# Spline-compressed FFN behind cross attention, one core: gate and up weights as one stationary matrix per tile, down cells in four classes, half of the rounding on ScalarE

## The chip, the core and the metric

The kernel runs on one core of one Trainium2 chip. The metric is the time of one execution on the device in microseconds (us). The kernel before takes 267.11 us, the median of three runs (267.0 to 267.25).

## What is computed

Four batches of 512 tokens with 512 columns. Each batch goes through an attention whose weights come from a context, and then through a feed-forward network whose three weight matrices are not stored: they are cubic (Catmull-Rom) interpolations of some 8000 control points each. Cut to what matters:

```python
x = x + xattn(layernorm(x), ctx, Wq, bq, Wk, bk)
#   query, key = ctx @ Wq.T + bq, ctx @ Wk.T + bk;  attention = softmax(query @ key.T)
#   xattn = layernorm(x) mixed by attention
gate_w = spline_reconstruct(gate_cp, 2048, 512)   # one control interval spans about 129 weights
up_w   = spline_reconstruct(up_cp, 2048, 512)
down_w = spline_reconstruct(down_cp, 512, 2048)
h = layernorm(x)
x = x + (silu(h @ gate_w.T) * (h @ up_w.T)) @ down_w.T
```

## The kernel before

All tensors are 128 partitions wide; a "tile" below is 128 of the 2048 inner rows (16 tiles, m = 0 to 15) by 512 tokens. The order of the work is written out by hand. One list of stages, `attention_only` and then `ffn(st, b, a)`, is run through once for each engine, and an engine issues its own part of each stage in that order. `ffn(b, a)` does the feed-forward network of batch b and, in between, the attention of batch a = b + 1. Between engines there are only semaphores; on one engine everything is first in, first out.

**Prologue.** `attention_only` makes the weights and does the attention of batch 0. An interpolated weight matrix is split into a smooth part of low rank ("nodes") and a residual that is not zero only near the breaks of the spline. The residual is a product of a small matmul (`spread`, L1209 to L1227) with precomputed tables: `residual` on VectorE multiplies two banks with two tables (L876), on GpSimd adds the two products (L1049). This gives gu_r for gate and up (8 steps, 512 wide) and d_r for down (8 steps of two tiles, 2 x 192 wide). `node_weights` (L1257, L717, L896) gives the node part gu_v. The table of down is loaded only when the gate and up residuals are done (L615).

**Gate and up, `gate_up(b, m)`.** Each of the two sums of a tile takes two matmuls: the residual weights against 128 columns of h (L1327) and 102 rows of node weights against zg, the projection of h on the node functions (L1330). ScalarE applies Silu out of the PSUM bank (`activate`, L776), VectorE multiplies with the up bank (L964), GpSimd rounds the product to fp32r for the down matmuls (`round_inter`, L1124). Gate and up have two banks each: gate(m) waits for the Silu of m - 2, up(m) for the product of m - 2.

**The projection.** `project` (L1306, L762, L952) makes zp from h; `replicate` (L1313, L769, L956) spreads it once to zg.

**Down.** `down_basis` (L1344) and `gather_halves` (L1356) take the node part, `down` (L1372) the residual part: per tile and token quarter one matmul of 128 rows against 192 columns. `down_tail` (L1379) adds the node part, and VectorE adds the result to x (L991).

**Attention inside `ffn`.** `energy` (L1192), `softmax` (maxima on VectorE L853, Exp on ScalarE L683), `scale` (L860), `prob_t` (transposes, L1236), `split_prob` (L703, L883). `split_x` splits the transposed input into xh (ScalarE, L709) and xl (VectorE, L887); `xm` (48 matmuls, L1279 to L1281) waits for it. Then `add_xm`, `norm_t` (transposes, L1294), and `cast_t`: ScalarE copies a bank to SBUF (L752), VectorE makes a rounded copy of that (L945). `project` of the next batch waits for all four ScalarE copies (L1301).

The stretch of `ffn` from the last tiles on, in the order in which all engines take it:

```python
st.activate(b, 15); st.round_inter(b, 15)
st.split_prob(a, 3); st.split_x(a)
st.down(b, 0, range(0, 12)); st.down_basis(b, 1); st.down(b, 0, range(12, 13))
st.down_basis(b, 2); st.half_split(b)
st.down(b, 0, range(13, 16)); st.down(b, 1, range(0, 16))
st.stats(a); st.xm(a, 0)
```

## Time and profile before

| | |
|---|---|
| median of three runs | 267.11 us |
| span of the profiled execution, first to last instruction | 265.8 us |
| TensorE matmuls busy | 247.6 us, 93% |
| VectorE | 188.2 us, 71% |
| GpSimd | 132.2 us, 50% |
| ScalarE | 123.6 us, 46% |
| start of `project`, batches 0 to 3 | 65.47, 119.68, 172.80, 225.92 us |

The profiled execution has no time of its own beside its span; the median of the runs is 1.3 us longer than the span, for what lies before the first and behind the last instruction. PE is TensorE, DVE is VectorE, ACT is ScalarE, POOL is GpSimd. A row of a timeline has the start, the duration, the engine, the line and the operation; "x2" is two instructions merged, with the time from the start of the first to the end of the last; in brackets stands the idle time of the engine before it and what ended it. Since consecutive instructions of an engine overlap at their ends, the distance from start to start is less than a duration.

### The profile page before, as it was taken

The page shows a single profiled execution, that of the slowest core. Times are in us where ns is not written, and L with a number is a line of the kernel's source. Part 1 is how long each engine was busy: PE and PEld are TensorE (multiplying, and loading weights), DVE is VectorE, ACT ScalarE, POOL GpSimd, SP SyncE. Part 2 cuts the span into 40 slices and gives each one's busy share as a digit, 9 for nine tenths or more (in the row PEclk, how much of TensorE's full clock was granted, in tenths as well). Part 3 has the DMA queues.
Part 4 walks back from the last instruction along what each step waited for, and adds up shares of the span by engine and source line. Part 5 has one row for each costly group of instructions (what it writes and reads, how often), then busy time and mean ns, then how long its engine had stood idle before and what let it go on. Part 6 is the DMA issues. An engine that isn't in the chain of part 4 may idle for free.

```text
span 265.8 us, 4144 instructions
## 1 busy us (share of the span) xinstructions
PE 247.6 (93%) x1400; PEld 171.8 (65%) x1400; DVE 188.2 (71%) x332; ACT 123.6 (46%) x206; POOL 132.2 (50%) x138
## 2 busy tenths in 40 slices
PE   7879649999899999999999999999999999599995
PEld 2223136855475868884858788848586888286684
DVE  0598996698778776866788768667887686465533
ACT  3035542325469652336696523366965233254320
POOL 0398717186883831314939313149393131487800
PEclk9968977999999999999999999999999999889999
DMA  6999107000091000022720000227000002200004
GB/s 184 335 427 419 42 16 297 6 0 2 0 353 44 2 1 2 0 79 79 276 118 0 0 0 0 79 79 296 20 0 0 0 0 79 79 2 0 0 2 158
DMA packets 7355, 23.11 MB, mean 87 GB/s; under 512 B 1201, under 2 KB 2481, under 8 KB 5937
## 3 DMA queue, kind: packets, MB, share of 16 engines
q1 hardware_dynamic: 7344, 22.98, 23.1%
q8 instruction: 6, 0.10, 0.1%
q14 instruction: 5, 0.03, 0.1%
HBM read 18.78 MB, written 4.19 MB: 86 GB/s over the span
## 4 chain that ended last, share of the span: by engine, by line
PE 79%; DVE 10%; ACT 3%; DMA 2%; issue 2%; POOL 1%; SPq 1%; DVEq 0%; POOLq 0%
PE bank L1327 12%; PE bank L1330 12%; PE bank L1372 11%; PE bank L1344 6%; PE bank L1174 5%; PE bank L1279 5%; PE bank L1281 5%; PE bank L1280 5%; DVE prod L876 4%; PE bank L1379 3%; PE bank L1236 3%; PE bank L1192 3%; DMA power<-in_g_power 2%; PE bank L1294 1%; PE bank L1356 1%
## 5 line engine op out<-in xcount | busy, mean ns | idle before, releaser
L1124 POOL TENSOR_TENSOR ih<-inter,ones 128x512 fp32r<-128x512 f32 x64 | 65.0, 1042 | 21.5 <-DVE inter L964 21.4
L964 DVE TENSOR_TENSOR inter<-inter,bank 128x512 f32<-128x512 f32 x64 | 43.7, 686 | 18.1 <-ACT inter L776 14.9
L776 ACT ACTIVATE inter<-bank 128x512 f32<-128x512 f32 x64 | 37.9, 598 | 23.7 <-PE bank L1330 23.6
L1372 PEld LDWEIGHTS bank<-d_r,ih 128*128 128x128 f32 x256 | 31.0, 191 | 7.8 <-issue 5.9
L1372 PE MATMUL bank<-d_r,ih 128*128 128x192 f32 x256 | 32.2, 276 | 0.0
L747 ACT ACTIVATE qk<-bank,nmr,rstd 128x512 f32<-128x512 f32 x16 | 12.5, 780 | 36.7 <-PE bank L1281 19.7
L1327 PE MATMUL bank<-xh,gate_r 128*128 128x512 f32 x64 | 27.6, 431 | 1.5 <-DVE zg L956 1.5
L1111 POOL TENSOR_TENSOR xres<-x,ones 128x2048 f32<-128x2048 f32 x4 | 14.4, 3602 | 24.0 <-DMA out<-xres 23.7
L1330 PE MATMUL bank<-zg,up_v 102*128 102x512 f32 x64 | 25.9, 404 | 0.0
L1327 PE MATMUL bank<-xh,up_r 128*128 128x512 f32 x64 | 25.7, 402 | 0.0
L1330 PE MATMUL bank<-zg,gate_v 102*128 102x512 f32 x64 | 25.6, 400 | 0.0
L1279 PE MATMUL bank<-ph,xh 128*128 128x512 f32 x64 | 25.2, 394 | 0.0
L1281 PE MATMUL bank<-ph,xl 128*128 128x512 f32 x64 | 25.0, 390 | 0.0
L1280 PE MATMUL bank<-pl,xh 128*128 128x512 f32 x64 | 24.9, 390 | 0.0
L1095 POOL TENSOR_TENSOR ve<-mv,eps 128x1 f32<-128x1 f32 x16 | 5.6, 349 | 30.0 <-DVE mv L937 30.0
L752 ACT ACTIVATE prob<-bank 128x512 f32<-128x512 f32 x16 | 8.7, 596 | 21.2 <-PE bank L1294 21.2
L1327 PEld LDWEIGHTS bank<-xh,gate_r 128*128 128x128 f32 x64 | 12.4, 194 | 9.5 <-DVE zg L956 4.1
L1158 PE MATMUL bank<-warm 128*128 128x512 bf16 x60 | 16.5, 429 | 1.5 <-DVE warm L811 1.5
L1174 PE MATMUL bank<-ctxT,wqk 128*128 128x512 f32 x32 | 17.2, 671 | 0.0
L1344 PE MATMUL bank<-inter,d_u 64*32 64x512 f32 x256 | 16.5, 598 | 0.0
L932 DVE TENSOR_TENSOR x<-x,qk 128x512 f32<-128x512 f32 x16 | 11.1, 695 | 6.7 <-ACT qk L747 6.7
L1330 PEld LDWEIGHTS bank<-zg,up_v 102*128 102x128 f32 x64 | 12.4, 194 | 3.8 <-ACT prob L683 1.1
(108 smaller groups left out, 454.1 us busy)
## 6 DMA issues: line engine op xcount, KB each, us to landing
x<-in_x SPq DMA_DIRECT2D x4, 1024.0 KB, 5.1
xT<-in_xT SPq DMA_DIRECT2D x4, 1024.0 KB, 7.1
out<-xres SPq DMA_DIRECT2D x16, 256.0 KB, 2.1
ctxT<-in_ctxT SPq DMA_DIRECT2D x4, 512.0 KB, 7.6
rd<-in_d_r SPq DMA_DIRECT2D x2, 768.0 KB, 6.1
knots<-in_d_knot SPq DMA_DIRECT2D x1, 1280.0 KB, 11.7
d_coef<-in_d_coef SPq DMA_DIRECT2D x1, 1024.0 KB, 14.6
d_pt<-in_d_node SPq DMA_DIRECT2D x1, 1024.0 KB, 16.0
```

What stands on the lines that cost most here:

```text
L776: nc.scalar.activation(inter[:, m], gbank[m % 2][:], ACT.Silu).then_inc(s["silu_done"], 1)
L964: V.tensor_tensor(inter[:, m], inter[:, m], ubank[m % 2][:], ALU.mult).then_inc(s["mult_done"], 1)
L1124: G.tensor_tensor(ih[:, m], inter[:, m], ones[:, 0].broadcast_to([P, TOK]), ALU.mult).then_inc(s["ih_done"], 1)
L1158: mm(zdbank[:], warm[:, 0:P], warm[:], start=True, stop=True)
L1174: last = mm(abank[n][:], wqk[:, n, c], ctxT[:, c], start=c == 0, stop=c == CTX // P - 1)
L1279: mm(abank[t % 2][:], xh[:, n, c], ph[:, n], start=n == 0, stop=False)
L1280: mm(abank[t % 2][:], xh[:, n, c], pl[:, n], start=False, stop=False)
L1281: last = mm(abank[t % 2][:], xl[:, n, c], ph[:, n], start=False, stop=n == NT - 1)
L1327: mm(dst[m % 2][:], gu_r[n][:, c, w * P:(w + 1) * P], xn2r[:, c], start=True, stop=False)
L1330: mm(dst[m % 2][:], gu_v[n][:, i], zg[:], start=False, stop=True).then_inc(s[done], 1)
L1344: last = mm(dst[QUAD * w:QUAD * (w + 1)], d_u[part, ORDER[m]], inter[part, m], start=m < CLS, stop=m >= MT - CLS, skip_group_check=True)
L1372: mm(in_blocks(obank[t][:], i // CLS), ih[:, m, t * P:(t + 1) * P], d_r[:, i], start=m == 0, stop=False, skip_group_check=True)
```

## The change

- **Gate and up.** The hidden columns are sorted into eight classes of 64 instead of four of 128. The stationary matrix of a tile is 128 rows: 64 rows of residual weights and 60 rows of node weights together (gw), against a moving matrix mv of the same two halves. So a tile takes two matmuls instead of four.
- **Moving side.** The halves of mv are filled by `cast_t` (a second ScalarE copy of half the partitions per bank, a VectorE copy of the other half) and by `replicate`, which now runs four times a batch: each time two matmuls, a ScalarE copy and two VectorE operations on 64 partitions. `replicate` 0 and 1 stand ahead of the tiles, 2 behind tile 3, 3 behind tile 7 and ahead of the softmax.
- **Rounding.** Odd tiles are rounded on ScalarE (`round_odd`, behind the Silu of the next even tile), even tiles on GpSimd.
- **xl** is computed on GpSimd (`low_x`), not on VectorE.
- **Down.** Four classes of cells instead of eight; a tile's blocks are 8 x 36 = 288 columns instead of 4 x 48 = 192. Tiles go in natural order.
- **Prologue.** Each gate and up residual is one VectorE product of 512 instead of two, and two GpSimd sums of 256; each down residual is one VectorE product of 2 x 288 for one tile (16 instead of 8 steps with two products each) and one GpSimd sum of 288. The residual table of down is loaded with the others, with no wait. The order of the stages is written anew.

```diff
@@ ffn
             st.project(b)
             if a is not None:
-                st.qk(a)
-            else:
-                st.replicate(b)
-            for m in range(4):
-                st.activate(b, m)
+                st.qk(a, 0)
+            for t in range(2):
+                st.replicate(b, t)
+            if a is not None:
+                st.qk(a, 1)
             for m in range(4):
                 st.gate_up(b, m)
+                st.activate(b, m)
                 st.round_inter(b, m)
+            st.replicate(b, 2)
             for m in range(4, 8):
+                st.gate_up(b, m)
                 st.activate(b, m)
-                st.gate_up(b, m)
                 st.round_inter(b, m)
+            st.replicate(b, 3)
             if a is not None:
                 for t in range(NT):
                     st.energy(a, t)
@@ ffn, behind the last tile
                 st.split_prob(a, 3)
                 st.split_x(a)
+                st.low_x(a)
             st.down(b, 0, range(0, 12))
@@ sync
-            sp.wait_ge(s["res_mul"], 4 * CLS)
-            load(rd2[:], "d_r2", "rd_in")
-            load(rd3[:], "d_r3", "rd_in")
+            load(rd[:].rearrange("p m k n -> p (m k n)"), "d_r", "rd_in")
@@ ScalarE
                 def cast_t(b, t):
                     act.wait_ge(s["xn2T_mm"], NT * b + t + 1)
-                    nc.scalar.activation(xn2T[:, t], abank[t % 2][:], ACT.Copy).then_inc(s["xn2t_copied"], 1)
+                    nc.scalar.activation(xn2T[:, t], abank[t % 2][:], ACT.Copy).then_inc(s["xn2t_first"], 1)
+                    nc.scalar.activation(mv[half(1), 2 * t + 1], abank[t % 2][half(1)], ACT.Copy).then_inc(s["xn2t_copied"], 1)
+                def replicate(b, t):
+                    act.wait_ge(s["zg_mm"], CLS * b + t + 1)
+                    if t >= 2:
+                        act.wait_ge(s["zg_done"], 2 * (CLS * b + t - 1))
+                    nc.scalar.activation(zs[:, t % 2], zbank[t % 2][:], ACT.Copy).then_inc(s["zg_hi"], 1)
                 def activate(b, m):
                     act.wait_ge(s["g_mm"], MT * b + m + 1)
                     nc.scalar.activation(inter[:, m], gbank[m % 2][:], ACT.Silu).then_inc(s["silu_done"], 1)
+                    if m >= 2 and m % 2 == 0:
+                        Stages.round_odd(b, m - 1)
+                def round_odd(b, m):
+                    act.wait_ge(s["mult_done"], MT * b + m + 1)
+                    nc.scalar.activation(ih[:, m], inter[:, m], ACT.Copy).then_inc(s["ih_odd"], 1)
                 def round_inter(b, m):
-                    pass
+                    if m == MT - 1:
+                        Stages.round_odd(b, m)
@@ VectorE
                 def split_x(b):
-                    dve.wait_ge(s["xh_done"], b + 1)
-                    V.tensor_tensor(xl[:], xT[:], xh[:].bitcast(f32), ALU.subtract).then_inc(s["xsplit_done"], 1)
+                    pass
-                def replicate(b):
-                    dve.wait_ge(s["zg_hi"], b + 1)
-                    V.scalar_tensor_tensor(zg[:], zg[:].bitcast(f32), g_low[:, 0:1], zgbank[0:G_K, :], ALU.mult, ALU.add).then_inc(s["zg_done"], 1)
+                def replicate(b, t):
+                    dve.wait_ge(s["zg_hi"], CLS * b + t + 1)
+                    for n in range(2):
+                        part = half(1 - n)
+                        V.scalar_tensor_tensor(mv[part, 2 * t + n], zs[part, t % 2].bitcast(f32), z_low[part], zbank[t % 2][part], ALU.mult, ALU.add).then_inc(s["zg_done"], 1)
@@ GpSimd
+                def low_x(b):
+                    pool.wait_ge(s["xh_done"], b + 1)
+                    G.tensor_tensor(xl[:], xT[:], xh[:].bitcast(f32), ALU.subtract).then_inc(s["xsplit_done"], 1)
                 def round_inter(b, m):
+                    if m % 2:
+                        return
@@ TensorE
                 def gate_up(b, m, a=None):
-                        mm(dst[m % 2][:], gu_r[n][:, c, w * P:(w + 1) * P], xn2r[:, c], start=True, stop=False)
                         if n == 1 and a is not None:
                             pe.wait_ge(s["exp_done"], NT * (a + 1))
-                        mm(dst[m % 2][:], gu_v[n][:, i], zg[:], start=False, stop=True).then_inc(s[done], 1)
+                        mm(dst[m % 2][:], gw[:, n, m // 2, m % 2 * P:(m % 2 + 1) * P], mv[:, m // 2], start=True, stop=True).then_inc(s[done], 1)
                 def down(b, t, tiles):
-                        mm(in_blocks(obank[t][:], i // CLS), ih[:, m, t * P:(t + 1) * P], d_r[:, i], start=m == 0, stop=False, skip_group_check=True)
+                        mm(in_blocks(obank[t], m % PHASES), ih[:, m, t * P:(t + 1) * P], d_r[:, m], start=m == 0, stop=False, skip_group_check=True)
```

## Rows read from the trace of the kernel before

**Rows 1.** The page: busy time of each engine, share, instructions.

```profile
PE 247.6 (93%) x1400; PEld 171.8 (65%) x1400; DVE 188.2 (71%) x332; ACT 123.6 (46%) x206; POOL 132.2 (50%) x138
```

**Rows 2.** Windows: length, busy time of each engine, PEclk; a whole batch, tiles 0 to 7.

```profile
119.68:172.80 53.12, 53.07 (x319) 39.51 (x319) 39.41 (x71) 29.16 (x49) 24.68 (x27) 1.00 0.18 69
124.90:132.55 7.65, 7.65 (x33) 6.32 (x34) 5.48 (x8) 5.30 (x9) 7.29 (x7) 1.00 0.58 222
```

**Rows 3.** Timeline, ahead of and in the first tiles of batch 1.

```profile
124.08 0.74 DVE L956 SCALAR_TENSOR_TENSOR zg<-zg,masks,bank 102x512 fp32r<-102x512 f32 x1
124.88 0.50 PE L1327 MATMUL bank<-xh,gate_r 128*128 128x512 f32 x1
...
126.58 0.60 ACT L776 ACTIVATE inter<-bank 128x512 f32<-128x512 f32 x1 [0.33 <-PE bank L1330]
...
127.22 0.69 DVE L964 TENSOR_TENSOR inter<-inter,bank 128x512 f32<-128x512 f32 x1 [0.21 <-ACT inter L776]
...
127.52 0.60 ACT L776 ACTIVATE inter<-bank 128x512 f32<-128x512 f32 x1 [0.34 <-PE bank L1330]
```

**Rows 4.** Timeline, the softmax of batch 2 and the Silu behind it.

```profile
132.74 1.28 ACT L683 ACT_TABLE_LOAD   x1
133.36 2.68 DVE L853 TENSOR_REDUCE nmax<-bank 128x1 f32<-128x512 f32 x4
...
136.88 1.28 ACT L776 ACT_TABLE_LOAD   x1
...
138.18 1.08 ACT L776 ACTIVATE inter<-bank 128x512 f32<-128x512 f32 x2
```

**Rows 5.** Timelines by engine, from the last product to the first matmul of xm.

```profile
147.05 0.69 DVE L964 TENSOR_TENSOR inter<-inter,bank 128x512 f32<-128x512 f32 x1 [0.55 <-ACT inter L776]
...
147.39 1.91 ACT L709 ACTIVATE xh<-xT 128x2048 fp32r<-128x2048 f32 x1
...
149.33 2.29 DVE L887 TENSOR_TENSOR xl<-xT,xh 128x2048 fp32r<-128x2048 f32 x1 [1.00 <-ACT xh L709]
...
152.63 0.42 PE L1279 MATMUL bank<-ph,xh 128*128 128x512 f32 x1
```

**Rows 6.** Groups by form: busy us, mean ns of one, idle before.

```profile
L1124 POOL TENSOR_TENSOR ih<-inter,ones 128x512 fp32r<-128x512 f32 x64 | 65.0, 1042 | 21.5 <-DVE inter L964 21.4
...
L1111 POOL TENSOR_TENSOR xres<-x,ones 128x2048 f32<-128x2048 f32 x4 | 14.4, 3602 | 24.0 <-DMA out<-xres 23.7
...
L876 DVE TENSOR_TENSOR prod<-bank,rd 128x384 f32<-128x384 f32 x16 | 7.9, 548 | 0.0
...
L876 DVE TENSOR_TENSOR prod<-bank,r2g 128x512 f32<-128x512 f32 x8 | 5.5, 686 | 1.7 <-PE bank L1221 0.9 <-DMA r2g<-in_g_r 0.8
...
L1071 POOL TENSOR_TENSOR d_coef<-d_coef,d_pt 128x512 f32<-128x512 f32 x4 | 5.0, 1266 | 0.0
```

**Rows 7.** Chain of waits in order of time (start, us): energy, 16 down matmuls.

```profile
132.55 2.77 PE bank L1192 x12
...
164.66 1.76 PE bank L1372 x16
```

**Rows 8.** Timeline, the last copies ahead of project, and project.

```profile
171.66 1.09 ACT L752 ACTIVATE prob<-bank 128x512 f32<-128x512 f32 x2 [0.48 <-PE bank L1294]
...
172.80 1.06 PE L1306 MATMUL bank<-prob,g_basis 128*32 128x512 f32 x8
```

**Rows 9.** TensorE timeline, end of the prologue: last spread, project of batch 0.

```profile
65.03 0.51 PE L1226 MATMUL bank<-knots,spread 128*128 128x192 bf16 x4 [0.40 <-DVE prod L876]
65.47 1.07 PE L1306 MATMUL bank<-prob,g_basis 128*32 128x512 f32 x8
```

**Rows 10.** Windows in the prologue, columns as in the windows above.

```profile
12.00:16.00 4.00, 2.37 (x9) 0.74 (x10) 3.14 (x6) 0.78 (x2) 3.75 (x4) 0.94 0.98 400
16.00:20.00 4.00, 4.00 (x6) 1.25 (x5) 4.00 (x8) 1.84 (x3) 4.00 (x4) 0.50 1.03 430
```

**Rows 11.** Chain of waits, last batch: the first down matmuls.

```profile
249.29 1.32 PE bank L1372 x12
```

More of the change, by code:

```diff
@@ L136, in constants @@
 def constants():
[L138 removed]
+    cell, hidden, reach, rows, tiles, knot, start, nodes, down = layout()
     c, at = {}, {}
[L140 to L150 removed]
@@ L382, in attention_only @@
             st.powers(0)
-            for r in range(2):
+            for r in range(4):
+                st.spread(r)
                 st.residual(r)
@@ L467, in attention_only @@
             st.norm_t(0, 1)
-            st.spread(13)
+            for r in range(18, 20):
+                st.spread(r)
             st.norm_t(0, 2)
```

704 lines of the change are left out of this document (372 added, 332 removed).

## The prediction

> **What bounds the kernel now.** I read the page's busy shares first, then windows over one whole batch, then the timelines engine by engine, and last the chain of waits. TensorE is busy for 93% of the span [rows 1]; from one project to the next, 53.12 us, it is busy for 53.07, while VectorE has 39.4, ScalarE 29.2 and GpSimd 24.7 [rows 2]. So in the three looped batches TensorE sets the time. In tiles 0 to 7 the Silus start 0.94 us apart, each with about 0.33 idle before it [rows 3]: four matmuls of about 0.23 us, in agreement with twelve energy matmuls in 2.77 [rows 7]. GpSimd's rounding takes 1.04 us a tile [rows 6] and is hardly slower. What the reader has to see is that behind TensorE stands no free engine but a chain Silu, product, rounding, whose links are all above half a tile's time.
>
> **What TensorE is spared.** Per batch 32 matmuls of 0.23 go, 7.4 us. Six more for replicate come, 1.4 us. The 64 down matmuls grow from 192 to 288 columns. Sixteen of 192 take 1.76, 0.110 each, and 512 columns take 0.231 [rows 7]. A straight line through both gives 0.146 for 288, in proportion to the 512 it is 0.130, and it can't be below 0.110; I take 0.14, nearer to the line, so +0.03 each (0 to 0.036), 1.9 us a batch. Net TensorE is spared 4.1 us a batch. The question is what is late next.
>
> **Tiles: the rounding on ScalarE closes a loop.** ScalarE's order is now Silu(odd), Silu(even), round(odd), Silu(next odd). round(odd) waits for the product of the same tile. A Silu takes 0.60, the product follows 0.04 later and takes 0.69 [rows 3], and another 0.04 goes to the hand-over: round(odd) can't start before 1.37 us after the start of Silu(odd). Then ScalarE needs its own start-to-start time until the next odd Silu: two Silus take 1.08 together, so 0.48, with 0.49 taken below [rows 4]. Together 1.86 us for two tiles, 0.93 a tile, against 0.94 now [rows 3]. What is queued behind the wait is every further Silu, and TensorE waits for that: so 7.4 us of matmuls less a batch buy nothing in the tiles. The cover that the four matmuls gave is replaced by an equal one.
>
> **What comes on top, per batch, from the first tile to xm.** VectorE's operations follow one another at 0.66: four maxima take 2.68, (2.68 - 0.69) / 3 [rows 4]; its two-step form takes 0.74 [rows 3].
> 1. Before the first tile two half-width operations replace one (64 partitions don't shorten them), so gate 0 starts 0.7 later; two more, of replicate 1, stand ahead of the first product. Part of that was idle time of VectorE: Silu 0 is 0.4 late, the first product about 1.1.
> 2. Behind tile 3 replicate 2 puts one ScalarE copy (0.49) and two VectorE operations (1.3) into the loop. Written out queue by queue, tile 7 is then 1.5 us late (0.9 if the VectorE part finds a gap).
> 3. Replicate 3 stands in VectorE's queue ahead of the maxima: 1.3 more. The Exps, ScalarE's table load of 1.28 and Silu 8 [rows 4] follow the maxima, so tile 8 is 2.8 us late.
> 4. Tiles 8 to 15: ScalarE has 8 Silus, 5 roundings and 4 copies of split_prob, 17 x 0.49 = 8.3 us as a bound. From Silu 8 (138.18) to the last product (147.05) it is now 8.9 [rows 4, 5]. With the loop's waits I get 8.4, so 0.5 is won. Here the spared matmuls do pay, but ScalarE takes nearly all.
> 5. xh starts 0.34 after the last product starts [rows 5]. Now ScalarE must wait for that product (0.69), then round tile 15 and copy ph: about 1.7 after. +1.4.
> 6. xl on GpSimd instead of 2.29 on VectorE [rows 5]. GpSimd takes 1.27 for 512 of two full operands, and 1.04 and 3.60 for 512 and 2048 where one operand is a single repeated value [rows 6]; the latter two leave 0.19 fixed. So 2048 with two operands is 4 x (1.27 - 0.19) + 0.19 = 4.5 us (bounds 3.6 and 5.1). +2.2.
> 7. Now xl is done at 151.62 and xm starts at 152.63 [rows 5]: 1.0 of slack is used up.
> The sum 2.8 - 0.5 + 1.4 + 2.2 - 1.0 is 4.9 us later for xm. Behind xl in GpSimd's queue stand only the small operations for rstd of the next batch, which add_xm needs at the end of the first quarter of xm, 2.7 us later: hidden. The eight roundings that GpSimd is spared (8 x 1.04) win nothing, because it waited for products anyway. TensorE's own work before xm (32 down matmuls, basis) is done some 2.5 us earlier than xl, which also hides its longer down matmuls. Bounds 3.7 and 5.5.
> The Trainium skill ("GPSIMD Engine Reference", "Elementwise") lists 4497 ns for a tensor_tensor of 2048 on GpSimd against 2293 ns on VectorE; the second agrees with the row of 2.29, and the first would leave this sum as it is.
>
> **Behind xm.** 32 down matmuls on the path, +1.0 (0 to 1.2). In cast_t each ScalarE copy gets a second one behind it, and the transposes of quarters 2 and 3 wait for the second copies of 0 and 1, project for the second of 3. Today the last copy ends at 172.75 and project starts at 172.80 [rows 8]: no slack. Three copies of 0.49 stand in the way, less about 0.1 of gap: +1.35 (0.5 if only the last is seen).
>
> So a looped batch gets 4.9 + 1.0 + 1.35 = 7.25 us longer (4.2 to 8.1), three of them 21.8.
>
> **Prologue.** The gate and up products go from 16 to 8, which shortens an early part that also waits for loads and GpSimd; I count -1 at the start of xm. Behind xm VectorE's chain of down products sets project: the last spread waits for it [rows 9]. Sixteen of 384 at 548 ns become 16 of 576; 512 take 686 [rows 6], so 576 take about 0.75, and 14 of them lie there: 14 x 0.2 = +2.8. The second cast copy hides partly. GpSimd's d_r sums of 288, at 0.8 to 1.1, end about when tile 0 needs them. On SyncE's queue the table of down now stands ahead of the loop's loads and behind all others; it waited until mid-prologue before, so nothing that is needed sooner comes later. Together +2 (-1.5 to +4).
>
> **Last batch.** No softmax, xh or xm. The tiles go from a loop of four matmuls to one of 0.93, the start is 0.7 later, the first down matmul (now at 249.29 [rows 11]) stays, and 64 down matmuls add 1.9; little hides them: +1.8 (0 to 3.5).
>
> **Sum.** 2 + 21.8 + 1.8 = 25.6 on a span of 265.8, so 291.4, and with the 1.3 that the median of 267.1 has beyond the span, 292.7. I say 292.5. With all lower bounds -1.5 + 12.6 + 0 = 11, 278; with all upper 4 + 24.3 + 3.5 = 32, 299.
>
> **Rivals.** (a) TensorE's clock falls. In 12 to 16 us TensorE is busy for 2.37 of 4, the granted clock still 0.94; from 16 to 20 it is 0.50, the lower level of 1.2 GHz [rows 10]. In the new tiles TensorE has 0.46 of 0.93 us to do, as thin. For it speaks that stretch; against it that the new one has a matmul pair every 0.93 us and no long gap. In the tiles even matmuls of 0.43 (two per tile, 0.86) fit into 0.93. The price comes behind them: energy (2.77) and the first basis (some 1.9) at half clock, partly hidden by VectorE, +2.5 us a batch and 2 once: 302. The Trainium skill ("TensorE: Matmul & The Clock Gate", "A second HAM failure mode: psum-queue depth-cycling") describes just this, many micro-idles between groups of matmuls that make the clock oscillate; by that rule this rival would be the forecast, but the looped batch of before is at 1.00 throughout [rows 2] and can't show it.
> (b) The queues fit better than I wrote them out: each VectorE insertion falls into a gap, xh is ahead, xl costs 3.6. Then ScalarE's busy time is the bound and a batch gets about 3 us longer: 267.1 + 9 + 2 + 1.8 = 280, down to 273 without the prologue's part and with down matmuls at 0.12.
> (c) Faster: TensorE stays the bound. If round(odd) finds its product always ready (ScalarE then has 1.47 us for two tiles) and xl ends before the down matmuls do, the spared 4.1 us a batch come through, four times: 267.1 - 16.4 = 251. It decides by the pair of tiles: below 1.86 us the change gains. Against it stands the order of ScalarE's queue together with durations that are all measured.
> (d) Gains and losses cancel to within what can be told: 267.
>
> **How the numbers follow.** Forecast 292.5, chance 0.63, with its own range 281 to 300. (a) 0.12, (b) 0.13, (c) 0.10, (d) 0.02. The range 273 to 302 leaves out (c), (d) and the upper part of (a), some 0.18. A run of this kernel can tell a change from none at about 0.2%. Faster (c) 0.11, same 0.02, slower 0.87.
>
> **What would show it.** Right: Silus 0.93 apart in tiles 0 to 7 with ScalarE waiting for VectorE's product ahead of the odd roundings; TensorE busy per batch down by 4 while the batch is at about 60.4; Silu 8 at 21.3 us after project's start instead of 18.5 (138.18 - 119.68) [rows 2, 4]; GpSimd's xl at 4.5 with TensorE idle 2 us ahead of xm; project waiting for ScalarE's second copy. Wrong: a batch below 53 us would speak for (c), a PEclk below 1.00 in the tiles or in the energy matmuls for (a). The step most likely to be off is the size of items 4 to 6, since it adds waits in three queues by hand.

## The result and the profile after

The changed kernel takes 319.1 us (median of four runs, 318.3 to 321.6) where the kernel before takes 267.1: 1.195 times as long, 95% interval 1.189 to 1.202. I had forecast 292.5 and a range up to 302. The direction was right, the size was half of what came.

First the page of the changed kernel, the line of busy shares that answers to [rows 1].

```profile
PE 248.7 (79%) x1320; PEld 156.2 (49%) x1320; DVE 205.8 (65%) x348; ACT 153.3 (48%) x261; POOL 122.9 (39%) x126
```

TensorE went from 93% of the span to 79%, and no other engine came near its place. So one has to go by stages. The starts of `project` cut the span:

| stretch | before | after | longer by | forecast |
|---|---|---|---|---|
| prologue, to project of batch 0 | 65.47 | 83.73 | 18.3 | 2 |
| batch 1 | 54.21 | 63.93 | 9.7 | 7.25 |
| batch 2 | 53.12 | 63.96 | 10.8 | 7.25 |
| batch 3 | 53.12 | 62.32 | 9.2 | 7.25 |
| last batch, to the end of the span | 39.9 | 42.2 | 2.3 | 1.8 |
| span | 265.8 | 316.1 | 50.3 | 25.6 |

Of the 24.7 us that I missed, 16.3 lie in the prologue and 7.9 in the looped batches. Windows of the changed kernel (length, then busy time of PE, PEld, DVE, ACT, POOL, and PEclk), whole batches to set beside [rows 2], then the first tiles of the third:

```profile
83.73:147.66 63.93, 53.51 (x294) 35.48 (x293) 44.68 (x80) 36.51 (x64) 23.50 (x23) 0.97 0.13 50
147.66:211.62 63.96, 54.44 (x292) 36.79 (x292) 42.14 (x77) 37.21 (x64) 21.25 (x20) 0.95 0.15 57
211.62:273.94 62.32, 52.08 (x293) 35.28 (x293) 42.06 (x77) 37.15 (x64) 21.26 (x20) 1.00 0.13 51
...
217.62:226.62 9.00, 6.26 (x21) 3.60 (x22) 8.16 (x13) 6.79 (x13) 3.20 (x4) 1.00 0.60 233
```

PEclk is 1.00 in one of the three batches only, and that one is 1.6 us shorter. In its first tiles VectorE is busy for 8.16 of 9.00 us and ScalarE for 6.79, which points at VectorE and not at ScalarE (experiment 11 tests it). The timeline of both there (start, us, engine, line; what stood before it):

```profile
219.82 2.02 DVE L1025 TENSOR_TENSOR inter<-inter,bank 128x512 f32<-128x512 f32 x3
...
221.12 0.63 ACT L834 ACTIVATE ih<-inter 128x512 fp32r<-128x512 f32 x1 [1.07 <-DVE inter L1025]
...
222.27 0.69 DVE L1025 TENSOR_TENSOR inter<-inter,bank 128x512 f32<-128x512 f32 x1 [0.43 <-ACT inter L828]
...
222.99 1.53 DVE L1017 SCALAR_TENSOR_TENSOR mv<-zd,masks,bank 64x512 fp32r<-64x512 f32 x2
...
224.44 2.02 DVE L1025 TENSOR_TENSOR inter<-inter,bank 128x512 f32<-128x512 f32 x3
```

Four products and the two half-width additions of `replicate` come round every 4.62 us (224.44 - 219.82), 1.15 us a tile instead of 0.94 [rows 3], and VectorE is busy for 4.2 of them. ScalarE sits idle 1.07 ahead of its rounding. The end of the same batch, in the place of [rows 5, 8]:

```profile
244.05 1.90 ACT L759 ACTIVATE xh<-xT 128x2048 fp32r<-128x2048 f32 x1
...
246.03 4.57 POOL L1127 TENSOR_TENSOR xl<-xT,xh 128x2048 fp32r<-128x2048 f32 x1 [2.58 <-ACT xh L759]
...
250.66 0.50 PE L1357 MATMUL bank<-ph,xh 128*128 128x512 f32 x1 [2.24 <-POOL xl L1127]
...
272.67 0.60 ACT L804 ACTIVATE prob<-bank 128x512 f32<-128x512 f32 x1
273.30 0.59 ACT L805 ACTIVATE mv<-bank 64x512 fp32r<-64x512 f32 x1
...
273.94 0.64 PE L1384 MATMUL bank<-prob,g_basis 128*32 128x512 f32 x4 [1.12 <-ACT mv L805]
```

GpSimd's xl at 4.57 and TensorE idle 2.24 ahead of xm are as forecast. Of the casts the reader is to see the distance: a full copy and the half-width one behind it start 0.63 apart, two full ones 0.49 (1.09 for two [rows 8]).

The prologue is where the size was missed. Timeline of VectorE and GpSimd in the changed kernel, then TensorE and what it waits with:

```profile
31.44 4.49 POOL L1127 TENSOR_TENSOR xl<-xT,xh 128x2048 fp32r<-128x2048 f32 x1
...
33.18 6.96 DVE L973 SCALAR_TENSOR_TENSOR win<-win 64x512 f32<-64x512 f32 x1
...
35.89 5.36 POOL L1142 TENSOR_TENSOR d_coef<-d_coef,d_pt 128x512 f32<-128x512 f32 x4
39.55 1.71 POOL L1142 TENSOR_TENSOR d_coef<-d_coef,d_pt 128x512 f32<-128x512 f32 x1
...
40.06 1.74 DVE L974 SCALAR_TENSOR_TENSOR knots<-knots 64x512 f32<-64x512 f32 x1
...
69.96 0.55 DVE L1056 TENSOR_SCALAR xT<-x,mv,rstd 128x512 f32<-128x512 f32 x1 [0.71 <-POOL rstd L1168]
...
72.49 4.59 PE L1231 MATMUL bank<-warm 128*128 128x512 bf16 x15
...
77.46 1.42 DVE L933 TENSOR_TENSOR prod<-bank,rd 128x576 f32<-128x576 f32 x2 [3.81 <-PE bank L1299]
77.60 1.09 PE L1372 MATMUL bank<-masks,xT 128*128 128x128 f32 x8
```

One operation of VectorE (L973, a step of the down knots' jumps) that takes 0.67 us in experiment 2 lasts 6.96 here, to the end of xl and past three of the four down taps on GpSimd; the next (L974) lasts 1.74 instead of 0.68. Together that is 7.4 of the 7.95 us by which the first xm is late (52.63 instead of 44.68). The last of the four taps, which the row at 39.55 shows by itself, took 1.71 where the first three took 1.26. And behind xm, 15 warm-up matmuls, whose results nobody reads, stand for 4.6 us ahead of the transposes of h, whose last input was ready at 70.5, and of spread 16, for which VectorE waits 3.81 us.

### The profile page after: what moved, and what is told of

Read it like the earlier page. It is cut to its first block, busy times and chain, and to the rows that moved or that the text cites. A ratio compares the mean times of both kernels' runs of the same rounds, so it can differ in the third digit from the quotient of the medians.

```text
span 316.1 us, 4063 instructions
## 1 busy us (share of the span) xinstructions
PE 248.7 (79%) x1320; PEld 156.2 (49%) x1320; DVE 205.8 (65%) x348; ACT 153.3 (48%) x261; POOL 122.9 (39%) x126
## 4 chain that ended last, share of the span: by engine, by line
PE 39%; DVE 20%; ACT 18%; issue 11%; POOL 8%; DMA 1%; SPq 1%; DVEq 0%; ACTq 0%; POOLq 0%
PE bank L1451 7%; DVE inter L1025 5%; PE bank L1357 5%; ACT inter L828 4%; POOL xl L1127 4%; PE bank L1359 4%; PE bank L1358 4%; DVE mv L1017 4%; PE bank L1423 3%; PE bank L1409 3%; ACT prob L804 3%; PE bank L1231 2%; PE bank L1458 2%; ACT mv L805 2%; DVE win L973 2%
## 5 line engine op out<-in xcount | busy, mean ns | idle before, releaser
L1409 PE MATMUL bank<-mv,gw 128*128 128x512 f32 x128 | 48.0, 470 | 18.8 <-DVE inter L1025 10.9
L1197 POOL TENSOR_TENSOR ih<-inter,ones 128x512 fp32r<-128x512 f32 x32 | 33.3, 1040 | 67.8 <-DVE inter L1025 67.8
L1025 DVE TENSOR_TENSOR inter<-inter,bank 128x512 f32<-128x512 f32 x64 | 42.5, 682 | 11.3 <-ACT inter L828 10.1
L1409 PEld LDWEIGHTS bank<-mv,gw 128*128 128x128 f32 x128 | 23.9, 202 | 43.6 <-DVE inter L1025 19.5
L1451 PEld LDWEIGHTS bank<-d_r,ih 128*128 128x128 f32 x256 | 35.4, 188 | 7.8 <-issue 6.7
L1451 PE MATMUL bank<-d_r,ih 128*128 128x288 f32 x256 | 38.1, 299 | 0.0
L1357 PE MATMUL bank<-ph,xh 128*128 128x512 f32 x64 | 25.6, 400 | 6.7 <-POOL xl L1127 6.7
L1017 DVE SCALAR_TENSOR_TENSOR mv<-zd,masks,bank 64x512 fp32r<-64x512 f32 x32 | 23.9, 747 | 3.9 <-ACT zd L821 3.0
L834 ACT ACTIVATE ih<-inter 128x512 fp32r<-128x512 f32 x32 | 20.2, 630 | 11.7 <-DVE inter L1025 11.7
L991 DVE TENSOR_TENSOR x<-x,qk 128x512 f32<-128x512 f32 x16 | 11.3, 706 | 17.3 <-ACT qk L799 17.3
L1127 POOL TENSOR_TENSOR xl<-xT,xh 128x2048 fp32r<-128x2048 f32 x4 | 18.2, 4551 | 7.7 <-ACT xh L759 7.7
L1299 PE MATMUL bank<-knots,spread 64*128 64x288 bf16 x32 | 6.6, 314 | 17.6 <-DVE knots L981 11.6
L940 DVE TENSOR_TENSOR pl<-bank,ph 128x512 fp32r<-128x512 f32 x16 | 11.0, 690 | 10.1 <-ACT ph L755 10.1
## 6 DMA issues: line engine op xcount, KB each, us to landing
d_coef<-in_d_coef SPq DMA_DIRECT2D x1, 1024.0 KB, 17.5
```

What stands on the lines that cost most here:

```text
L1017: V.scalar_tensor_tensor(mv[part, 2 * t + n], zs[part, t % 2].bitcast(f32), z_low[part], zbank[t % 2][part], ALU.mult, ALU.add).then_inc(s ...
L1025: V.tensor_tensor(inter[:, m], inter[:, m], ubank[m % 2][:], ALU.mult).then_inc(s["mult_done"], 1)
L1127: G.tensor_tensor(xl[:], xT[:], xh[:].bitcast(f32), ALU.subtract).then_inc(s["xsplit_done"], 1)
L1197: G.tensor_tensor(ih[:, m], inter[:, m], ones[:, 0].broadcast_to([P, TOK]), ALU.mult).then_inc(s["ih_done"], 1)
L1357: mm(abank[t % 2][:], xh[:, n, c], ph[:, n], start=n == 0, stop=False)
L1409: mm(dst[m % 2][:], gw[:, n, m // 2, m % 2 * P:(m % 2 + 1) * P], mv[:, m // 2], start=True, stop=True).then_inc(s[done], 1)
```

## The experiments

All totals stand beside runs of the kernel before on the same chip, 267.1 to 268.1.

**1. The wait in the prologue: VectorE first.** GpSimd's xl waits until VectorE's jumps are done.

```diff
 def low_x(b):
+    if first(b):
+        pool.wait_ge(s["jump_split"], 2)
     pool.wait_ge(s["xh_done"], b + 1)
```

> The changed kernel, with one wait added in the prologue: GpSimd starts xl of batch 0 and the down taps behind it only when VectorE's jumps are done. Theory A (a VectorE operation with two SBUF operands can't proceed while GpSimd works through its own tensor operations): L973, which took 6.96 us in the changed kernel, falls back to about 0.7, L974 from 1.7 to 0.7, the scale of the softmax starts some 7 us sooner, and the whole is 7 us shorter, about 312. Rival B (the long operation comes from its 64-partition shape or from the loads that land at the same time): L973 stays near 7 us and the time near 319.

VectorE and GpSimd in the same stretch:

```profile
38.65 4.50 POOL L1129 TENSOR_TENSOR xl<-xT,xh 128x2048 fp32r<-128x2048 f32 x1 [4.26 <-DVE knots L981]
...
38.82 8.81 DVE L916 TENSOR_SCALAR prob<-prob,rinv 128x512 f32<-128x512 f32 x4
43.11 5.64 POOL L1144 TENSOR_TENSOR d_coef<-d_coef,d_pt 128x512 f32<-128x512 f32 x4
```

L973 is back at 0.67, but the four scalings behind it now take 8.81 instead of 1.68. The wait had only moved to the next VectorE operations without a PSUM operand (the shape and the loads of rival B are out), and xm came no earlier (53.88), so the gain of 7 us that theory A forecast did not come. The total says nothing, as its runs scatter from 319 to 329.

**2. The same with GpSimd out of the way altogether.** xl of the prologue waits for VectorE's last scaling, and the taps stand behind xl in GpSimd's queue.

```diff
 def low_x(b):
+    if first(b):
+        pool.wait_ge(s["prob_done"], NT)
```

> The changed kernel, with GpSimd's first xl and its down taps held until VectorE's last softmax scale of the prologue, so that they run beside no VectorE work that has both inputs in SBUF. Theory A, contention: a VectorE operation that reads SBUF alone waits for a whole back-to-back stretch of GpSimd, and this costs what it cost in whichever place the two meet. Then here no such operation is stretched: the jumps (lines 973, 974) take 0.7 us each, the four tensor_scalar 0.42 us each, the first xm stands at 47 to 50 us instead of 52.6, and the total falls by 2 to 5 us, to 314 to 317; the rest of the prologue's +18 stays, as it lies behind the first xm. Rival B, the critical path ahead of the first xm is GpSimd's own work (its taps, 5.4 us, are needed by the down matrix): then the first xm comes earlier but the project stage does not, and the total stays within 1.5 us of 319.

```profile
33.50 0.67 DVE L973 SCALAR_TENSOR_TENSOR win<-win 64x512 f32<-64x512 f32 x1
...
37.17 1.67 DVE L916 TENSOR_SCALAR prob<-prob,rinv 128x512 f32<-128x512 f32 x4
```

Neither the jumps nor the scalings are stretched any more, and the first xm starts at 45.54, 7.1 us earlier. `project` comes only 4.2 earlier (79.53), because xm itself took 16.3 us instead of 13.6, at a granted clock of 0.90. The total is 316.1 (1.185, 1.176 to 1.195), which is in theory A's range, with the rest of the prologue's loss untouched.

**3. The same costs in isolation.** A row of operations on idle engines behind the last output of the kernel before; of each kind one is shown.

```diff
+    nc.scalar.activation(inter[part, 4 + n], bank[n % 2][part], ACT.Copy)
+    V.scalar_tensor_tensor(inter[part, 12 + n], x[part, n], eps[part, 0:1], bank[2 + n % 2][part], ALU.mult, ALU.add)
+    G.tensor_tensor(inter[:, 4 * n:4 * n + 4], xT[:], x[:], ALU.mult)
+    V.tensor_tensor(prob[:, 2], x[:, 2], x[:, 3], ALU.mult)
+    V.tensor_scalar(prob[:, 3], x[:, 3], eps[:, 0:1], None, ALU.mult)
```

> The kernel before, with a row of operations on idle engines behind the last output, for their durations alone. ScalarE: four full-width copies 128x512 from PSUM, four that alternate between full width and one half (64 partitions), two of the same half. VectorE: four scalar_tensor_tensor at full width, four alternating between the two halves, four of the same half; then, beside two back-to-back GpSimd tensor_tensor 128x2048, in order a tensor_tensor with one input in PSUM (twice), bn_stats from SBUF, a tensor_tensor with both inputs in SBUF; and beside two more, a tensor_scalar from SBUF and a tensor_tensor with one in PSUM. Theory A, a change of partition range between neighbours ends the overlap of one operation with the next: full width at a pitch of 0.60 to 0.66 us on VectorE and 0.49 to 0.54 on ScalarE, alternating halves 0.75 to 0.80 and 0.62, the same half again 0.60 to 0.66 and 0.49 to 0.54. Rival B, half width as such is the slow form: the same half takes 0.75 to 0.80 and 0.62 as well. Contention, theory A: with PSUM as an input the operation keeps its 0.6 to 0.7 us beside GpSimd; with both inputs in SBUF it takes 5 to 9 us, or else GpSimd's takes longer than its 4.6; bn_stats and tensor_scalar from SBUF: if the shared port is held by GpSimd for its whole stretch, 5 us or more, if only two-input operations meet it, 0.4 to 0.7.

```profile
262.77 2.06 ACT L806 ACTIVATE inter<-bank 128x512 f32<-128x512 f32 x4 [6.49 <-DVE xres L1004]
262.77 2.72 DVE L1009 SCALAR_TENSOR_TENSOR inter<-x,eps,bank 128x512 f32<-128x512 f32 x4
264.69 2.45 ACT L809 ACTIVATE inter<-bank 128x512 f32<-128x512 f32 x4
265.41 3.02 DVE L1012 SCALAR_TENSOR_TENSOR inter<-x,eps,bank 64x512 f32<-64x512 f32 x4
267.05 1.06 ACT L811 ACTIVATE ctxT<-bank 64x512 f32<-64x512 f32 x2
268.45 2.71 DVE L1014 SCALAR_TENSOR_TENSOR prob<-x,eps,bank 64x512 f32<-64x512 f32 x4
...
271.63 9.41 POOL L1180 TENSOR_TENSOR inter<-xT,x 128x2048 f32<-128x2048 f32 x2
271.71 1.29 DVE L1018 TENSOR_TENSOR prob<-x,bank 128x512 f32<-128x512 f32 x2 [0.54 <-POOL spare L1178]
272.92 0.69 DVE L1019 BATCH_NORM_STATS2 bst<-x 128x6 f32<-128x512 f32 x1
273.52 3.17 DVE L1020 TENSOR_TENSOR prob<-x 128x512 f32<-128x512 f32 x1
...
281.23 4.69 DVE L1022 TENSOR_SCALAR prob<-x,eps 128x512 f32<-128x512 f32 x1 [4.54 <-POOL spare L1182]
```

Half width: the same half four times over takes 2.71 us, no more than full width (2.72); alternating halves take 3.02, 0.10 us for each of the three changes. On ScalarE four full ones take 2.06 and four that go full, half, full, half 2.45. (L809 is shown by the shape of its first.) So theory A: not the narrow form is slow, the change of partitions between neighbours is. Beside GpSimd: an input in PSUM (L1018) and bn_stats (L1019) are not touched; with both inputs in SBUF (L1020), or as a tensor_scalar from SBUF to SBUF (L1022), VectorE waits until GpSimd's instruction ends. Neither of the two expectations for one-input operations fits both, since bn_stats goes free and tensor_scalar waits; and with 3.17 and 4.69 us both waits end with GpSimd's first instruction of two, short of the 5 to 9 us expected.

**4. Rounding back on GpSimd.** In the changed kernel, ScalarE rounds nothing.

```diff
 def activate(b, m):   # ScalarE
-    if m >= 2 and m % 2 == 0:
-        Stages.round_odd(b, m - 1)
 def round_inter(b, m):   # GpSimd
-    if m % 2:
-        return
```

> The changed kernel with all rounding on GpSimd again. Theory A (the loop Silu, product, rounding on ScalarE sets the tiles): Silus in tiles 0 to 7 come closer than in the changed kernel (8.0 us from Silu 0 to Silu 7 in the last looped batch), to 6 or 6.5, xh starts about 2.5 us sooner because no product and rounding stand ahead of it, and a batch is 3 to 4 us shorter: about 308 in all. Rival B (VectorE's replicate operations set the tiles, the rounding stands in gaps): Silu 0 to 7 stays above 7.5 and a batch is shorter by less than 1.5, only through xh: above 314.

Measured 313.7 (1.174, 1.165 to 1.184): batches of 61.1, 60.8 and 61.6 us, between the two expectations. Silu 0 to Silu 7 takes 7.5 us instead of 8.0 at full clock, but from project to energy it is 14.8 instead of 14.95, as rival B had it. The gain lies behind: from Silu 8 to xh it takes 8.9 to 9.0 us, where batches 1 and 2 of the changed kernel have 11.5 and 11.2, at granted clocks of 0.81 to 0.88 in all of these.

**5. xl back on VectorE** in batches 1 to 3.

```diff
 def split_x(b):   # VectorE
+    if not first(b):
+        V.tensor_tensor(xl[:], xT[:], xh[:].bitcast(f32), ALU.subtract)
```

> The changed kernel with xl of batches 1 to 3 on VectorE again (batch 0 as changed). Theory A (xm waits for xl at the end of a chain, GpSimd's 4.57 us against 2.29): xm starts 2.2 us sooner after project, TensorE's wait ahead of it falls from 2.2 us to nearly 0, three batches give 6 to 7 us: about 312.5. Rival B (xl is hidden by TensorE's own down matmuls to the greater part): gain below 3 us in all.

Measured 314.3 (1.176, 1.169 to 1.183): batches of 61.7, 61.4 and 61.4. From xh to xm it takes 4.28 us instead of 6.60, theory A in its size; the total gained 4.8 instead of 6 to 7, with no batch at full clock here where the changed kernel has one.

**6. The second cast copy on VectorE.**

```diff
 def cast_t(b, t):
-    nc.scalar.activation(mv[half(1), 2 * t + 1], abank[t % 2][half(1)], ACT.Copy)
+    V.tensor_copy(mv[half(1), 2 * t + 1], xn2T[half(1), t])
```

> The changed kernel, with the second copy of each cast_t tile made by VectorE from xn2T (SBUF to SBUF) instead of by ScalarE from PSUM. Theory A, ScalarE's eight casts per batch are on the path behind xm: the stretch from xm to the project falls by 1.0 to 1.5 us a batch (23.3 to about 22), and the total by 4 to 6 us, to 313 to 315. Rival B, the path behind xm is set by norm_t on VectorE and TensorE's transposes: the stretch stays at 23.3, or grows by 4 x 0.3 us as VectorE has four more copies, and the total is 318 to 323.

Two answers. In the looped batches the stretch from xm to project fell from 23.3 to 21.0, more than theory A said, and the whole of it lies between the transposes and project: 3.36 us where the changed kernel has 5.61 and the kernel before 3.35. But the total is 320.7 (1.201, 1.195 to 1.207), in the range of rival B though not for its reason. Project of batch 0 came 3.1 us later (86.80): between the first xm and project VectorE has 23.2 us of work instead of 21.1. And batch 1 took 65.4 where the next two took 60.4 and 61.2. There one of the copies moved to VectorE, SBUF to SBUF, meets GpSimd:

```profile
89.33 3.60 POOL L1182 TENSOR_TENSOR xres<-x,ones 128x2048 f32<-128x2048 f32 x1 [0.26 <-POOL d_r L1114]
...
89.39 3.83 DVE L1003 CAST mv<-prob 64x512 fp32r<-64x512 f32 x1
```

It lasts 3.83 instead of 0.42 us, until GpSimd's copy of x is done, and the first Silu of the batch comes 12.8 us behind project instead of 6.9. This is the wait of experiments 1 to 3 in another place, made by the cure itself.

**7. The prologue's order in TensorE's queue.** Experiment 1, with spreads 10 and 11 moved behind xm(3), and the 15 warm-up matmuls ahead of spread 16 left out.

```diff
-for r in range(10, 12):
-    st.spread(r)
 st.xm(0, 3)
...
-for r in range(12, 14):
+for r in range(10, 14):
     st.spread(r)
...
-for t in range(15, 20):
-    st.keep_warm(t)
```

> As e1_jumps_first, and two more things in the prologue: spread 10 and 11 stand behind the last quarter of xm instead of ahead of it (with the products of VectorE moved alike), and the 15 filling matmuls ahead of spread 16 are gone. Theory A (TensorE's queue order holds xm 3 for 2.2 us, and the fill holds VectorE's products and the transposes for 4.5 us): project of batch 0 starts at about 70 instead of 83.7, total about 305. Rival B (VectorE's and GpSimd's chain of down products sets project, the fill only covers it): project not before 73, total above 308.

Measured 319.7 (1.194, 1.184 to 1.203), project of batch 0 at 82.52. From the first xm to project it takes 28.7 us instead of 31.1, and all of that lies within xm (11.3 us instead of 13.6), where spreads 10 and 11 no longer stand. From the end of xm to project it takes 17.4 us, and 17.5 in the changed kernel, at granted clocks of 0.71 and 0.90. The later batches took 63.1, 63.8 and 64.9. Theory A, project at about 70 and a total of 305, is out; the numbers are rival B's.

**8. All moves of work taken back at once.** xl on VectorE, all rounding on GpSimd, the cast copies on VectorE, the order of 7 (with the warm-up matmuls), and a wait of the taps for VectorE's last scaling. These are the diffs of 4 to 6 and 7 together, that wait, and xl of batch 0 as well:

```diff
-    if not first(b):
+    if True:
         V.tensor_tensor(xl[:], xT[:], xh[:].bitcast(f32), ALU.subtract)
```

What stays of the change is the merged matrix with its half-width copies, and the down product in four classes.

> The changed kernel with all of its load moves taken back or mended together: xl of every batch on VectorE, all rounding on GpSimd, the second cast copies on VectorE, the prologue's spreads 10 and 11 behind xm(3), GpSimd's taps held until VectorE's scale. What is left of the change is the merged gate and up matrix with its half-width copies, and the down product in four classes. Theory A, the moves add up: each alone gave 1 to 2.5 us a batch, together the batch falls from 62 to 64 us to 57 to 59, against 53.1 in the kernel before, and the total to 297 to 305, so that most of the loss per batch is the half-width work of the merged matrix itself. Rival B, they free the same slack: the batch stays at 60 to 61 (each alone gave 61.1 and 61.5), the total at 308 to 313. Rival C, the moves were the loss: the batch returns to 53 to 55 and the total to 275 to 288.

Measured 303.5 (1.136, 1.129 to 1.142), batches 2 and 3 of 57.8: theory A. One by one the three moves gave 2.8, 2.2 and about 3 us a batch (against 63.9 at the same clock, 0.97), together 6.1, so they share some slack. The shared part shows between xh and xm: 4.28 us with xl alone on VectorE, 5.79 here. Batch 1 is longer, 63.2, and so it is in experiment 9 (62.0): in both, one cast copy on VectorE lasts 3.8 us beside GpSimd's copy of x, as in experiment 6. Some 3.4 us could still be had there, an estimate from 3.83 - 0.42. Project still starts at 80.47.

**9. The same without the 15 warm-up matmuls.**

```diff
-for t in range(15, 20):
-    st.keep_warm(t)
 for r in range(16, 18):
     st.spread(r)
```

> The kernel with the load moves taken back (0, 303.5 us) without the 15 warm-up matmuls that stand in TensorE's queue ahead of spread 16 and of the first transposition behind xm. Theory A: in that kernel the transposition starts 9.3 us behind the normalised tile it reads, 4.3 of them under these matmuls; without them the first project comes 3.5 to 5 us earlier, at 75.5 to 77 us, and the total is 298.5 to 300.5. Rival B, VectorE's twelve down products, of which each pair waits for TensorE and GpSimd in turn, set the project's time: it comes less than 1.5 us earlier, total 302 to 303.5. Case C, without them the clock falls and takes back what they held: first batch over 63.5 us.

Measured 298.1 (1.117, 1.109 to 1.124). Project starts at 77.06, 3.4 earlier (0.6 of that already at the first xm), near theory A's 3.5, and the total gained 5.4, a little more than it said.

```profile
139.07:196.85 57.78, 52.49 (x293) 36.02 (x293) 45.67 (x82) 30.53 (x52) 24.58 (x27) 0.97 0.17 64
196.85:253.13 56.28, 50.96 (x293) 35.31 (x293) 45.67 (x82) 30.55 (x52) 24.50 (x27) 1.00 0.15 56
```

The windows of batches 2 and 3 are one program at two granted clocks: 1.5 us a batch is what the clock costs, as in the changed kernel (1.6).

**10. Two single moves on the kernel before.** First the rounding of the odd tiles on ScalarE, then xl of batches 1 to 3 on GpSimd.

```diff
+    nc.scalar.activation(ih[:, m], inter[:, m], ACT.Copy)   # first kernel, odd m
...
+    G.tensor_tensor(xl[:], xT[:], xh[:].bitcast(f32), ALU.subtract)   # second kernel, not first(b)
```

> The kernel before, with one edit of the change alone: the odd tiles rounded by ScalarE. Theory A, it is a loss in itself only where ScalarE is on the path: in the kernel before a tile takes TensorE 0.92 us and ScalarE would have 0.60 x 2 + 0.60 = 1.8 us for two tiles, just under it, so the first tiles keep their pitch and the last ones, which GpSimd held back at 1.04 us each, come no later: 266 to 269 us, a batch of 53.1 +- 0.7. Rival B, the hand-over (ScalarE waits for VectorE's product of the tile before) breaks the pitch: each pair of tiles takes 0.3 us more, 2 to 3 us a batch, 275 to 279.

> The kernel before, with xl of batches 1 to 3 on GpSimd alone. Theory A: xl takes 4.6 us instead of 2.3 and starts when GpSimd has rounded its last tile, about a microsecond after xh: it ends 1 to 3 us behind the last product of the down stage that TensorE can do without it, so xm comes 1 to 2.5 us later in each of three batches, and the total is 270 to 275. Rival B, the 2.3 us that VectorE gains in that stage are worth as much: 266 to 268.5.

Measured 268.9 (1.006, 1.004 to 1.009) with batches of 53.9, and 269.3 to 274.1 (1.010, 1.005 to 1.016 by the four fastest of six runs) with batches of 54.6. Both differences are small, but clear of the noise. Both theories A hold, the first with a batch 0.1 over its bound: 0.8 us a batch for the rounding, 1.4 for xl.

**11. Which engine bounds the tiles.** Two more operations a batch, ahead of tiles 2 and 5, into an unused buffer; once on VectorE, once on ScalarE.

```diff
+    if m in (2, 5):
+        V.tensor_tensor(scrap[:], inter[:, m - 2], ubank[m % 2][:], ALU.mult)
     V.tensor_tensor(inter[:, m], inter[:, m], ubank[m % 2][:], ALU.mult)
```

> The changed kernel with two more operations on VectorE in each batch, products of a full tile into an unused buffer ahead of tiles 2 and 5 (0.69 us each). Theory A, tiles 0 to 7 are bound by VectorE (four products of 0.69 and two half-width additions of 0.77 are 4.3 us for four tiles): the stretch from Silu 0 to the first energy product grows by 1.2 to 1.5 us a batch and the total by 4.5 to 6 us, to 323 to 326. Rival B, they are bound by ScalarE as the prediction had it: growth under 0.5 us a batch, 318 to 321.

> The changed kernel with two more operations on ScalarE in each batch, copies of a full tile from PSUM into an unused buffer ahead of the Silu of tiles 2 and 5 (0.60 us each). Theory A, VectorE is the bound and ScalarE has room: growth of the stretch from Silu 0 to the first energy product of 0 to 0.6 us a batch, total 318 to 322. Rival B, ScalarE is the bound: 1.0 to 1.3 us a batch, 323 to 325. Case C, the two are in one ring with TensorE's two banks, so that either's pad counts: then this one and VectorE's both give 1 us or more a batch.

From project to the first energy matmul the three looped batches grew by 3.1, 1.8 and 1.4 us with VectorE's pad (two of 0.69) and by 0.2, 1.8 and 0.6 with ScalarE's (two of 0.60). Most of this is not the pads: in the cases of 3.1 and of both 1.8, 1.7 to 2.4 us lie ahead of Silu 0, where no pad stands, at granted clocks of 0.69 and 0.79. So only the stretch from Silu 0 to Silu 7 is to be read, at equal clock (us, granted clock of the stretch in brackets):

| kernel | batch 1 | batch 2 | batch 3 |
|---|---|---|---|
| changed | 8.00 (1.00) | 8.63 (0.80) | 8.02 (1.00) |
| pad on VectorE | 8.69 (1.00) | 8.69 (1.00) | 9.25 (0.82) |
| pad on ScalarE | 8.00 (1.00) | 8.82 (0.81) | 8.61 (0.80) |

At full clock VectorE's two pads cost 0.69, ScalarE's nothing; at 0.80 to 0.82 it is 0.62 and 0 to 0.2. So VectorE bounds these tiles. Of its two pads the one ahead of tile 5 counts in full; the other delays its own product by 0.6 and the next by 0.1, so it fell into idle time. That is why the growth is half of what theory A said. The totals, 325.6 with VectorE's pad and runs scattered from 319 to 326 with ScalarE's, carry the clock's part too and are not read. Experiment 8 agrees: ScalarE has 5.63 us of work in 9.00 instead of 6.79 there, and the stretch from project to energy is 15.0 as before.

**12. The clock in the tiles.** Each gate and up matmul issued twice in the changed kernel, then the same on experiment 9.

```diff
+    mm(dst[m % 2][:], gw[:, n, m // 2, ...], mv[:, m // 2], start=True, stop=True)
     mm(dst[m % 2][:], gw[:, n, m // 2, ...], mv[:, m // 2], start=True, stop=True).then_inc(s[done], 1)
```

> The changed kernel with each of its gate and up matmuls issued twice (the second starts the sum anew, so the result is the same): 32 more matmuls of 0.23 us at full clock in a batch, in tiles that TensorE spends half idle. Theory A, TensorE's idle time between these tiles makes the clock fall, and the low clock costs what the changed kernel lost beyond the sum of its longer steps: the granted clock over tiles stays 1.00 instead of falling to 0.81 in some batches, no batch takes longer than 62.5 us, and the total falls by 2 to 6 us, to 313 to 317. Rival B, the matmuls only lengthen the path from VectorE's product to the next tile: 0.23 to 0.46 us a tile in 16 tiles, 4 to 7 us a batch, total 335 to 345. Between the two, the total within 2 us of 319: the clock is worth as much as the matmuls cost.

> Both of the last two edits on the kernel with the load moves taken back: no 15 warm-up matmuls, gate and up matmuls issued twice. If the clock is what is left between this kernel's batches (57.8 us, granted clock 0.97; the first 63.2 at 0.89) and the sum of its longer steps, the first batch falls to 58 to 60 and the total to 292 to 297. If the additional matmuls lie on the path, the batch grows to 61 or more, total over 308.

Measured 327.5 (1.222, 1.214 to 1.230) and 309.6 (1.158, 1.151 to 1.165). The granted clock over the first tiles was 1.00 in all three looped batches of both, where it had been 0.81 in the second of the changed kernel. It fell elsewhere in the first of the two kernels: in its batches 1 and 3 the stretch from xm to the transposes takes 19.2 us at 0.91 instead of 17.6. And batches at full clock are 63.8 instead of 62.3, and 59.6 instead of 56.3: the 32 matmuls cost 1.5 and 3.3 us a batch, at least what the clock is worth. None of the ranges expected for the first of them was met; of the second the total is over 308, as expected for matmuls on the path, with batches of 59.6 instead of 61 or more. The cure is no gain.

No combination came near the kernel before, so there is no version that beats both.

## Why the prediction was wrong

The batch at full clock, stage by stage (us, batch 3 of each):

| stretch | before | after | longer by | forecast | experiment 9 |
|---|---|---|---|---|---|
| project to energy | 12.70 | 14.95 | 2.25 | | 15.03 |
| energy to Silu 8 | 5.79 | 7.30 | 1.5 | 2.8 with the line above | 7.18 |
| Silu 8 to xh (items 4, 5) | 9.22 | 10.18 | 0.96 | 0.9 | 7.42 |
| xh to xm (items 6, 7) | 5.24 | 6.61 | 1.37 | 1.2 | 5.78 |
| xm to the transposes | 16.82 | 17.67 | 0.85 | 1.0 | 17.52 |
| transposes to project | 3.35 | 5.61 | 2.26 | 1.35 | 3.35 |
| batch | 53.12 | 62.32 | 9.2 | 7.25 | 56.28 |

**What held.** Items 4 to 7, of which I had called the sizes of 4 to 6 the likeliest to be off, came within 0.2 us: from Silu 8 to the last product it took 8.44 (8.4 forecast), xh started 1.74 behind that product (1.7), xl took 4.57 (4.5) and used up its slack, the down matmuls took 0.1325 (0.14).

**Tiles: the wrong engine.** I wrote ScalarE's loop out, got 0.93 us a tile, and hung replicate's operations on as separate delays. Measured are 1.15 a tile, by VectorE, which has 4 x 0.69 + 2 x 0.77 = 4.3 us in four tiles if one only adds up its queue. Items 1 to 3 come to 3.75 instead of 2.8. Experiment 11 shows the engine: at full clock a pad on VectorE counts and one on ScalarE does not. The taking back of the rounding left this stretch as it was (15.03). ScalarE was a limit in tiles 8 to 15: without the roundings the stretch from Silu 8 to xh falls from 10.2 to 7.4, below the 9.2 of before; experiment 4, which takes back nothing else, has the same fall at the lower clock (11.2 to 11.5 down to 9.0). That is the gain of the spared matmuls, and the moved rounding ate it.

**Casts: a term too small.** 2.26 instead of 1.35, shown by experiment 6, which brings the stretch back to 3.36. I had counted 0.49 for each added copy; they start 0.63 apart from the last, and the transposes of the next quarter wait for each in turn.

**Clock: a rival treated as an alternative.** I gave 0.12 to a falling clock, as a case in place of the forecast. It came on top, in two of three batches, for 1.4 and 1.6 us (2.5 forecast). It cost them in the tiles, where I had let the slow matmuls fit: 11.5 and 11.2 us from Silu 8 to xh instead of 10.2, and 0.6 in the first tiles of batch 2. (Batch 1 is longer by another 0.3 ahead of Silu 0, at full clock.) From energy to Silu 8, where I had put the price, all three took 7.30. The rule named there, from the Trainium skill ("TensorE: Matmul & The Clock Gate", "A second HAM failure mode: psum-queue depth-cycling"), agrees with the trace as far as the oscillation goes: TensorE idles 0.2 to 1.3 us between its pairs, and in the same stretch of three equal batches the granted clock was 1.00, 0.81 and 1.00.

**Prologue: the step that failed.** I gave it +2. It cost 18.3, which the trace divides by place into 7.95 before the first xm, 2.3 within xm and 8.0 behind it.

The first part is the wait at which I had put nothing: VectorE's operations out of SBUF stood behind GpSimd's, 8.7 us for two (L973, L974) that take 1.35. Experiment 2 takes 7.1 us back at xm, and 4.2 of them arrive at project. The second part (xm takes 13.6 us instead of 11.3) comes from spreads 10 and 11, which stand in TensorE's queue ahead of xm(3) and wait for VectorE; with them behind it xm takes 11.3 (experiments 7 and 8).

The third part is not wholly shown. From the first xm to project it takes 10.3 us longer than before. VectorE has 21.1 us of work there instead of 17.2: 15 down products take 10.9 us in place of 13 in 6.5. I had that term (+2.8 for 14), and 0.72 a product came close to my 0.75. The other 6.3 us are idle time of VectorE (10.0 instead of 3.6), for which I had counted nothing. The largest piece of it, 3.81, is the wait behind the 15 warm-up matmuls. They are no addition of the change. In the kernel before they stand in the same place and hide behind VectorE's last normalised tile:

```profile
57.82 3.40 PE L1158 MATMUL bank<-warm 128*128 128x512 bf16 x15
...
61.80 1.10 PE L1294 MATMUL bank<-masks,xT 128*128 128x128 f32 x8 [0.25 <-DVE xT L995]
```

In the changed kernel that tile was ready at 70.5, before TensorE had come to them (72.49). Leaving them out brings project 3.4 us earlier in experiment 9; in experiment 7, with two more spreads behind xm and a lower granted clock, the stretch behind xm did not shrink. So what they cost in the changed kernel itself, and how the rest divides between the granted clock (0.90 there, 1.00 before) and the ring spread, product, sum, is open.

The wait was there to be seen. In the kernel before, VectorE and GpSimd overlap in the prologue as well, and there GpSimd lost:

```profile
22.91 2.28 DVE L887 TENSOR_TENSOR xl<-xT,xh 128x2048 fp32r<-128x2048 f32 x1
23.13 3.20 POOL L1078 TENSOR_TENSOR win<-knots 128x512 f32<-128x512 f32 x1
...
26.30 1.27 POOL L1079 TENSOR_TENSOR win<-knots 128x512 f32<-128x512 f32 x1
```

L1078 takes 3.20 where its neighbour of the same shape, L1079, takes 1.27. The change put a longer run of GpSimd (xl and the taps, 9.8 us) beside VectorE's jumps, and I looked only at whether either engine had the time. The Trainium skill ("SBUF — State Buffer", "SBUF: two separate sides") says that the two engines share a pair of ports as an exclusive lock, held by an operation for the whole of its length, and names the VectorE forms that need it. The row of L1078 and every line of experiment 3 agree. By that rule alone the loss would end with GpSimd's running instruction, at 35.9; L973 ended at 40.14, past three more instructions.

## What to carry to other kernels

Add up every engine's queue over one period of the loop before following any single chain: here the sum per period would have named VectorE (4.3 us for four tiles). When work moves between VectorE and GpSimd, list for each side which operations have all their operands in SBUF and which of them now run beside each other; a price from a row that ran alone doesn't hold there. The same goes for a cure: the cast copies moved to VectorE paid 3.4 us at one new meeting of this kind (experiments 6, 8 and 9). A saving on the busiest engine is worth only what the next queues leave, stage by stage: the matmuls spared here paid 1.8 us in tiles 8 to 15 once nothing was moved into that stage, and nothing in tiles 0 to 7.

## What the hardware showed that I had not expected

- A VectorE operation that lies in SBUF alone waited for GpSimd: 6.96 us instead of 0.67 for one, 3.83 instead of 0.42 for a copy, 8.81 instead of 1.68 for four in a row. It doesn't always get in when GpSimd's instruction ends: L973 let three boundaries pass (the ends of xl and of two taps), while the operations of experiment 3 got in at the first (3.17 and 4.69 us). Why, no run here shows. bn_stats out of SBUF did not wait (0.69).
- Changing the half of the partitions from one operation to the next costs 0.10 us each time on VectorE (3.02 and 2.72 for four operations, three changes); staying in one half costs nothing (2.71). On ScalarE a change between full width and one half costs 0.13 (2.45 and 2.06).
- The granted clock of equal batches of one program differed (1.00, 0.95 and 0.97), for 1.4 to 1.6 us a batch.
